# One-hot tiles built on ScalarE, node rows in two float32r parts, and 24 of 52 columns fetched by TensorE

## What is computed

```python
# layer 0, first attention (per head)
e = leaky_relu(alpha_s[src] + alpha_d[dst], 0.2)
p = exp(e - segment_max(e, dst)[dst])
out = segment_sum(h[src] * (p / segment_sum(p, dst)[dst])[:, :, None], dst)
...
# layer 3, 90 edge types
h_src = h[src]
e = concatenate([h_src @ Ws.T, he @ Ws.T, h[dst] @ Ws.T], axis=1) @ Wa.T
msg = einsum('ei,eio->eo', h_src, W_rel[rel_type]) * e
h_out = segment_sum(msg, dst)
```

## Time and profile before

| | |
|---|---|
| median of 3 runs | 27713.97 us (27705.8 to 27721.58) |
| profiled execution | 27723.67 us, span 27721.6 us |
| first attention pass (800 columns per take), one chunk | from the first to the last of 62 scores: 883.1 to 4070.4 us |
| typed pass, one half | from the first to the last of 620 takes: 24222.5 to 27538.5 us |
| granted TensorE clock, mean | 0.91 |

### The profile page before, as it was taken

How to read it: one execution, slowest core, us unless ns; L and a number is a source line. 1 busy time by engine, 2 the same in 40 slices (tenths; PEclk the granted TensorE clock), 3 DMA queues, 4 the chain that set the end, 5 groups by cost and what they waited for, 6 DMA issues and landing times. The chain is left out here.

```text
span 27721.6 us, 477560 instructions
## 1 busy us (share of the span) xinstructions
PE 22581.0 (81%) x178452; PEld 17103.5 (62%) x178452; DVE 19269.3 (70%) x45474; ACT 1534.2 (6%) x3291; POOL 17285.6 (62%) x15844
## 2 busy tenths in 40 slices
PE   0788876888857999969999398889898897399996
PEld 0444433444426888858888388888888886155554
DVE  4788885555555777757777376676766765499996
ACT  0000000000000000000000011111111111100000
POOL 1555556666654555546655478888888888455555
PEclk9998987999977999979999699999999998599998
DMA  4222221111111111111111122222222222522221
GB/s 80 61 65 63 62 59 28 40 40 40 40 34 32 33 34 34 34 29 32 32 32 31 19 37 39 35 39 37 37 39 35 39 40 25 132 57 60 60 60 42
DMA packets 1658941, 1225.33 MB, mean 44 GB/s; under 512 B 1258202, under 2 KB 1501076, under 8 KB 1615348
## 3 DMA queue, kind: packets, MB, share of 16 engines
q0 software_dynamic: 870816, 181.33, 10.7%
q1 hardware_dynamic: 676628, 585.00, 7.7%
q10 hardware_dynamic: 110016, 437.07, 4.0%
HBM read 736.61 MB, written 465.15 MB: 43 GB/s over the span
## 5 line engine op out<-in xcount | busy, mean ns | idle before, releaser
L946 PE MATMUL gat_e_found<-gat_e_parts,gat_e_lowhot 128*128 128x400 bf16 (+1 forms) x30504 | 5867.6, 356 | 1077.8 <-DVE gat_e_rows L915 927.4
L2352 PE MATMUL sheaf_e_found<-sheaf_e_parts,sheaf_e_lowhot 128*128 128x238 bf16 x46872 | 5274.5, 274 | 939.5 <-DVE sheaf_e_lowhot L2164 462.4
L2113 POOL DMA_INDIRECT bysrc<-sheaf_e_toadd,sheaf_e_torow x3224 | 5162.4, 1601 | 1312.5 <-issue 758.2
L1027 POOL DMA_INDIRECT gat_e_rows<-att_t,gat_e_index x4464 | 4236.5, 949 | 2676.6 <-DMA gat_e_rows<-att_t,gat_e_index 1423.3
L2352 PEld LDWEIGHTS sheaf_e_found<-sheaf_e_parts,sheaf_e_lowhot 128*128 128x128 bf16 x46872 | 4688.9, 101 | 1370.0 <-issue 546.2
L750 POOL DMA_INDIRECT rgcn_e_rows<-rel_t,rgcn_e_index x3968 | 3753.8, 946 | 2844.5 <-DMA rgcn_e_rows<-rel_t,rgcn_e_index 1468.4
L946 PEld LDWEIGHTS gat_e_found<-gat_e_parts,gat_e_lowhot 128*128 128x128 bf16 x30504 | 3035.1, 100 | 3909.7 <-DVE gat_e_rows L915 996.3
L1843 PEld LDWEIGHTS rgcn_e_found<-rgcn_e_parts,rgcn_e_lowhot 128*128 128x128 bf16 x52080 | 5033.8, 99 | 559.4 <-issue 490.5
L1843 PE MATMUL rgcn_e_found<-rgcn_e_parts,rgcn_e_lowhot 128*128 128x224 bf16 x52080 | 5245.8, 264 | 78.9 <-issue 72.0
L2801 POOL DMA_INDIRECT typed_e_rows<-typed_t,typed_e_index x1984 | 1903.4, 959 | 1434.7 <-DMA typed_e_rows<-typed_t,typed_e_index 910.5
L946 PE MATMUL typed_e_found<-typed_e_parts,typed_e_lowhot 128*128 128x400 bf16 x14880 | 2686.0, 338 | 57.9 <-DVE typed_e_lowhot L890 57.9
(11 more groups left out here) (497 smaller groups left out, 22017.0 us busy)
## 6 DMA issues: line engine op xcount, KB each, us to landing
sheaf_e_allsrc<-src_d ACTq DMA_DIRECT2D x62, 1664.0 KB
sumsatt<-gat_e_sums ACTq DMA_DIRECT2D x62, 1404.0 KB
rgcn_e_low<-low_d SPq DMA_DIRECT2D x124, 640.0 KB
typed_e_types<-in_type_t SPq DMA_DIRECT2D x62, 1280.0 KB, 8.1
typed_t<-typed_p_y SPq DMA_DIRECT2D x98, 765.0 KB
gat_e_rows<-att_t,gat_e_index POOLq DMA_INDIRECT x4464
sheaf_e_low<-low_d SPq DMA_DIRECT2D x62, 1152.0 KB
sumsatt<-gat_e_sums ACTq DMA_DIRECT2D x62, 1092.0 KB
```

The lines of the kernel that those rows point to most:

```text
L946: last = pe.matmul(self.found_ps[n % 2][:, c, 0:self.width * self.cut.highs], hot[:, k, col * P:(col + 1) * P], self.table.column(part, k) ...
L1027: pool.indirect_dma_start(rows_t[a.k][:, j, :], None, table, rows(index[a.k][:, j:j + 1]))\
L2113: pool.indirect_dma_start(g.by_src[k][r], rows(to_row[k][:, j:j + 1]), to_add[k][:, j, 0:FD], None, compute_op=ALU.add).then_inc(summed[k] ...
L2352: last = pe.matmul(found_ps[n % 2][:, c, 0:W * NHI], hot[:, k, col * P:(col + 1) * P], short.column(part, k), start=part == 0 and k == 0, ...
```

## The change

`HelpedFinder` takes the place of `Finder` where the table has up to 512 columns, that is in the first attention pass and, as the parent of `TypedFinder`, in the typed pass.

- The one-hot tiles are made on ScalarE in two steps: for each of 4 tiles `away` = |lane - low| (ACTIVATE Abs, 128x512, float16), then one ACTIVATE Relu over all four, max(0, 1 - away), 128x2048, written as float32r. `prepare` on VectorE is then empty in the first pass and only builds the type's one-hot in the typed pass, with a semaphore of its own (`kind_built`), for which `look` waits.
- The table is cut in two float32r parts in place of three bf16 ones: a column is 2 x 4 = 8 matmuls with 400 columns.
- Both passes fetch 24 columns on TensorE (12 halves, 6 groups) and gather 28; the drains are then at columns 6, 12, 18 and 24.
- ScalarE's program is written out: build group 1, store the chunk before the last, exponential of the last chunk, build groups 2 to 5, build group 0 of the next chunk. Stores now wait for `done` of a chunk that is one chunk older than before.
- The 51 sums (41 in the second attention pass) are shared evenly over the steps.

```diff
--- before.py
+++ after.py
...
-    return Cut(FLO, FHI, g.few_low_d, g.few_high_d, 3, BF16)
+    return Cut(FLO, FHI, g.few_low_d, g.few_high_d, 2, F32R)
...
+class HelpedFinder(Finder):
+
+
+    def __init__(self, s, g, cut, sources, width, columns, rest=None):
+        super().__init__(s, g, cut, sources, width, columns, rest)
+        self.away = s.sb("away", [P, cut.tiles, QC * P], F16)
+        self.away_ready = s.sem("away_ready")
+
+    def prepare(self, dve, a, q, fresh=False):
+
+        return
+
+    def build_low(self, act, a, q, fresh=False):
+
+
+        G = a.c * self.groups + q
+        if q == 0:
+            act.wait_ge(self.low_in[a.k], a.turn * 16 + 16)
+        if not (fresh and q == 0):
+            act.wait_ge(self.low_built, G)
+        for n in range(self.cut.tiles):
+            last = act.activation(self.away[:, n, :], self.low[a.k][:, q * QC * P:(q + 1) * QC * P], ACT.Abs,
+                                  bias=self.g.low_f[:, n:n + 1], scale=-1.0)
+        last.then_inc(self.away_ready, 1)
+        act.wait_ge(self.away_ready, G + 1)
+        if not (fresh and q < 2):
+            act.wait_ge(self.found, 2 * G - 2)
+        act.activation(self.low_hot[(a.k * self.groups + q) % 2][:, :, :], self.away[:, :, :], ACT.Relu, bias=1.0,
+                       scale=-1.0).then_inc(self.low_built, 1)
+
+    def build_rest(self, act, a, qs, fresh=False):
+
+        for q in qs:
+            self.build_low(act, a, q, fresh)
...
-        f = Finder(s, g, quarters(g) if found_w * FHI <= 512 else sevenths(g), sources, found_w, columns)
+        helped = found_w * FHI <= 512
+        f = HelpedFinder(s, g, quarters(g), sources, found_w, columns) if helped else \
+            Finder(s, g, sevenths(g), sources, found_w, columns)
...
-                    share = -(-scans // (last_step - 1))
-                    for n in range((step - 2) * share, min(scans, (step - 1) * share)):
+                    steps = last_step - 1
+                    for n in range((step - 2) * scans // steps, (step - 1) * scans // steps):
...
-                f.build_low(dve, At(0, 0), 0, fresh=True)
+                f.prepare(dve, At(0, 0), 0, fresh=True)
...
+                def raise_(a):
+                    act.wait_ge(dropped, a.c + 1)
+                    act.activation(factor[:, :, :, :], drop[:, :, :, :], ACT.Exp).then_inc(raised, 1)
+
+                def store(a):
+                    act.wait_ge(done, a.c + 1)
+                    act.dma_start(chunk(acc, a.turn, a.k), sums[a.k][:, :, :]).then_inc(stored[a.k], 16)
+                    for t in by_edge_z:
+                        w = t.shape[1]
+                        act.dma_start(chunk(by_edge(t), a.turn, a.k),
+                                      zero[:, 0:J * w].rearrange("p (j w) -> p j w", w=w)).then_inc(zeroed, 16)
+
+                def turn(a, stores=True, last=False):
+                    f.build_low(act, a, 1)
+                    if stores:
+                        store(a.prev().prev())
+                    raise_(a.prev())
+                    f.build_rest(act, a, range(2, f.groups))
+                    if not last:
+                        f.build_low(act, a.next(), 0)
+                if helped:
+                    f.build_rest(act, At(0, 0), range(f.groups), fresh=True)
+                    f.build_low(act, At(0, 1), 0)
+                    turn(At(0, 1), stores=False)
+                    with act.Fori(1, NCH // 2 - 1) as i:
+                        for k in range(2):
+                            turn(At(i, k))
+                    turn(At(NCH // 2 - 1, 0))
+                    turn(At(NCH // 2 - 1, 1), last=True)
+                    store(At(NCH // 2 - 1, 0))
+                    raise_(At(NCH // 2 - 1, 1))
+                    store(At(NCH // 2 - 1, 1))
...
-class TypedFinder(Finder):
+class TypedFinder(HelpedFinder):
...
+    def wait_for_room(self, sp, built):
+        sp.wait_ge(self.kind_built, built)
+        sp.wait_ge(self.low_built, built)
...
-    def build_low(self, dve, a, q, fresh=False):
+    def prepare(self, dve, a, q, fresh=False):
...
-                          self.type_rows[a.k][:, q * QC * P:(q + 1) * QC * P], self.g.lane_f[:, :], None, ALU.is_equal)
-        super().build_low(dve, a, q, fresh)
+                          self.type_rows[a.k][:, q * QC * P:(q + 1) * QC * P], self.g.lane_f[:, :], None, ALU.is_equal)\
+            .then_inc(self.kind_built, 1)
...
+        if n % 2 == 0:
+            pe.wait_ge(self.kind_built, a.c * self.groups + n // 2 + 1)
...
+                def store(a):
+                    act.wait_ge(done, a.c + 1)
+                    act.dma_start(chunk(acc, a.turn, a.k), sums[a.k][:, :, :]).then_inc(stored[a.k], 16)
+
+                def turn(a, stores=True, last=False):
+                    f.build_low(act, a, 1)
+                    if stores:
+                        store(a.prev().prev())
+                    f.build_rest(act, a, range(2, f.groups))
+                    if not last:
+                        f.build_low(act, a.next(), 0)
+                f.build_rest(act, At(0, 0), range(f.groups), fresh=True)
+                f.build_low(act, At(0, 1), 0)
+                turn(At(0, 1), stores=False)
+                with act.Fori(1, NCH // 2 - 1) as i:
                     for k in range(2):
-                        a = At(i, k)
-                        act.wait_ge(done, a.c + 1)
-                        act.dma_start(chunk(acc, i, k), sums[k][:, :, :]).then_inc(stored[k], 16)
+                        turn(At(i, k))
+                turn(At(NCH // 2 - 1, 0))
+                turn(At(NCH // 2 - 1, 1), last=True)
+                store(At(NCH // 2 - 1, 0))
+                store(At(NCH // 2 - 1, 1))
...
-            attention_pass(nc, g, "gat1_e", h1, FD, 20, [g.h[:, :, :]], table1, g.expand["att1"], sums1,
+            attention_pass(nc, g, "gat1_e", h1, FD, 24, [g.h[:, :, :]], table1, g.expand["att1"], sums1,
...
-        typed_attention_pass(nc, g, "typed_e", 20, [g.h[:, :, :]],
+        typed_attention_pass(nc, g, "typed_e", 24, [g.h[:, :, :]],
```

34 lines of the change are left out of this document (16 added, 18 removed).

## The result

The changed kernel takes 27466.15 us (median of 4 runs, 27452.45 to 27474.13), the kernel before 27717.78 beside it (4 runs, 27705.8 to 27723.02): **0.9909 of the time before, 95% interval 0.9892 to 0.9926**, 252 us less. The prediction was 529 us less. The sign came as forecast and the first pass gave what was forecast of it; the typed pass and a pass outside the change did not, and the size is half.

What follows compares the result with a forecast made beforehand. POOL was taken to pace both passes; afterwards POOL and VectorE bound the first, VectorE the typed. Savings of 412, 110 and 7 us sum to 529, giving 27185 us; own range 27100 to 27280, wide range 27080 to 27520.

Steps and rivals of the forecast that it cites:

- First pass: First attention pass: POOL 45.5, VectorE 45.2 + 0.3, so 45.6 us a chunk in place of 52.25, 412 us less.
- a sign asked for under 80: First pass: VectorE's wait for gathers was to go down from 309 us to under 80.
- both: First pass after the change: POOL at 45.5 us and VectorE at 45.2 + 0.3 were both named as the bound.
- the account of before: Both passes before: POOL waits only for its own gathers and sets the pace, 52.4 and 53.2 us a chunk.
- float32r: TensorE matmuls of 400 columns in both passes: one pass over the columns, X = 0.17 us each.
- The first rival: TensorE: float32r streams two cycles a column, X = 0.35, TensorE becomes the bound, kernel 30080 us; chance 0.12.
- the second: TensorE: weight load not hidden, wholly or in part, 0.22 us a matmul, kernel 27540 us; chance 0.08.
- ScalarE: Building the one-hot tiles: 4.9 us per group, 29 per chunk, all beside other work.
- Typed pass: Pace goes from POOL to VectorE: 51.8 us a chunk in place of 53.57, 110 us less.
- not over 97: Typed pass: VectorE busy over 97% was a sign that the forecast holds.
- the prediction had 7: Once ahead of the typed pass: two-part table needs 4 copies and 4 subtractions fewer, about 7 us less.
- weight loads and drains: Rivals: weight load not hidden, 27540 us, chance 0.08; gathers not shorter because drains grow, 27310 us, chance 0.06.

## Why the prediction was right in kind and wrong in size

- **First pass: right.** 45.79 us against 45.6, with 393.9 us of the 412. The terms too: the score of 24 columns lasts 1.36 us, GpSimd's drains 692.0 us in 241 waits, 2.87 each (2.79 taken), VectorE's waits for gathers are gone (309 us before, a sign asked for under 80). Who sets the pace was left as "both"; it is VectorE, with GpSimd 0.5 us behind. One thing in the account of before was too simple: that GpSimd's own gathers and drains alone fix 52.25 and 53.57 us. With the same 32 gathers the periods fell to 50.00 and 52.04 once the rest of the change was in.
- **float32r: right.** 16 matmuls of the typed pass take 3.16 us and start 0.18 to 0.19 us apart (0.17 taken, 0.35 the rival's), 24 x 8 x 0.02 = some 4 us of TensorE a chunk more than the sum has, which cost nothing. The 0.17 was the bf16 price, 24 matmuls in 4.22 us or 0.169 us apart; that float32r would run at it was the author's estimate, which no row of before shows. The 4-byte weight load lasts 0.19 to 0.20 us on average, in f32 in the trace of before as in float32r in that of the change, for 0.10 in bf16, and lies beside the matmul ahead of it; the prediction had read up to 0.11 from the distance of two matmuls. The first rival is out, and the second at its price of 0.22 (its 42.6 us should be 192 x 0.22 = 42.2); whether the 0.02 are its loads is open.
- **ScalarE: right.** Four Abs in 2.56 us and a Relu in 1.92, 4.5 us a group (4.9 taken), 59% and 49% of the two windows.
- **Typed pass: the step that failed.** "Typed: VectorE 51.7 + 0.3 - 0.2 = 51.8" was the sum of what the instructions need, and that sum is right: 52.05 us with the loop placed, 93 us in all under the 53.57 of before. What it lacked is a term for reading the loop's code again, 2.6 us a chunk on the very engine that had just become the bound. With it the pass stands at 54.68, and VectorE is busy 91% of the window, not over 97 (96% with the loop placed). This is a term that was missing, not one mis-sized: the trace of before has no such stand, because that body of 310 recorded instructions stayed loaded in its place, and the sum took it, without saying so, that the new body would stay free of it.
- **The rest of the program: the second step that failed,** unspoken. The sum held every untouched pass at its old time. The sheaf pass took 104 us more: the new first pass has 16 matmuls a half where there were 24, so fewer of TensorE's instructions stand ahead of the sheaf loop, and its head slid to some 32 short of a block's end (told by the stop at the 33rd instruction, and by slot 224, which gives the kernel before the same stop and the same loss).
- **The books.** 162 us (typed) and 104 (sheaf) against the 271 us measured between the two profiled executions give 537, beside the 529 predicted. That they come so close is in part luck: 50 us of the 537 lie outside the two passes, where the prediction had 7, and make up for 18 us that the first and 17 that the typed pass fell short.
- **The range.** The forecast's own, 27100 to 27280 us, missed by 186 us. The wide one, 27080 to 27520, held the time by luck: its upper end was set by weight loads and drains, and neither brought it there. The chance of 0.71 for the forecast was too high for a change that moves code in a kernel whose traffic of instructions I had not looked at.

## What to carry to other kernels

Read the page's instruction queues before costing a change that alters the length of a program with long loops, and look for an engine that stands still right behind its branch: here that was a cost of place, and a slot (162.5 us in the typed pass) or a hint (161 us in the sheaf pass) took it away without touching the work. With VectorE as the bound its stands counted in full (162 us of them in the change, 162.5 won back); in the kernel before, where GpSimd sets the pace, about half did (50 of 108). Judge a change by both kernels placed alike; otherwise the difference contains the luck of either.

## What the runs showed of the hardware

- VectorE's typed loop in the change: its 304 recorded instructions stay loaded from slots 0 and 72, from slot 88 they don't (9 or 149 transfers of 8192 bytes in the pass). Where it is read again, the first take behind the branch comes 3.3 to 3.8 us late, and in the change there is a second stand, 8 recorded instructions on, of 2.6 us (66.4 in 26 waits). In the sheaf pass the stand at the branch is 4.8 to 6.1 us. TensorE's transfers are 16384 bytes.
- The hint for the branch takes VectorE's stand in the sheaf pass from 5.04 to 0.61 us and TensorE's from 2.9 us to none; on TensorE's relation loops it takes the transfers from 275 to 14 a pass.
- float32r on TensorE: 0.18 to 0.19 us for 400 columns, against 0.17 in bf16. As VectorE's result it makes a comparison of 512 elements 0.43 us long instead of 0.31.
- GpSimd's drains: of the five in a chunk of the kernel before, four last 2.2 to 2.3 us and the one across the seam 5.0 in nearly every chunk; with 20 columns and the rest of the change that one lasts 2.5. Why stays open.
